# Stacks of the heads interleaved by four rows: six transfers of 256 KB in place of twelve of 128 KB, and the maxima's two rows in their free rows

## What is computed

```python
x = x + tanh(g_xattn[0]) * L0_xattn(layernorm(x), ctx, ...)    # two-way attention and a gate
x = x + tanh(g_ffn[0])   * L0_ffn(layernorm(x), ...)           # one expert of eight for each position
x = x + tanh(g_xattn[1]) * L1_xattn(layernorm(x), ctx, ctx)    # 16 heads, below
x = x + tanh(g_ffn[1])   * L1_ffn(layernorm(x), ...)           # two experts of eight, gelu

q, k, v = (heads(z @ W.T + b) for z in (x, ctx, ctx))          # 16 heads of 16 features
q = q * cos + rotate_half(q) * sin;  k = k * cos + rotate_half(k) * sin
p = softmax(q @ k.T * 16 ** -0.5)
out = merge(p @ v) @ Wo.T + bo
```

## Time and profile before

| | us |
|---|---|
| median of three runs | 536.92 |
| lowest and highest of them | 531.25, 536.98 |
| the profiled execution's own time | 531.52 |
| its span, first to last instruction | 530.2 |
| TensorE busy with matmuls | 469.8 (89% of the span) |
| VectorE, ScalarE, GpSimd busy | 346.1, 335.1, 280.8 |
| mean granted clock of TensorE | 0.941 of full speed |

### The profile page before, as it was taken

The page is one execution under the profiler, slowest core; times in us unless marked ns, Lnnn a source line. Parts: engine busy times, 40 slices in busy tenths (PEclk is TensorE's granted clock), DMA queues, the critical chain, the costliest instruction groups (busy, mean ns, idle before and its releaser), DMA issues.

```text
span 530.2 us, 11126 instructions
## 1 busy us (share of the span) xinstructions
PE 469.8 (89%) x3888; PEld 413.9 (78%) x3888; DVE 346.1 (65%) x865; ACT 335.1 (63%) x691; POOL 280.8 (53%) x362
## 2 busy tenths in 40 slices
PE   3999999999999674767886799999999999999996
PEld 3999999999888573636664558788788888878896
DVE  5576676787567557552645676868656695976475
ACT  3388788876758223322254578878867768687833
POOL 2236564575533876445366756837668184423154
PEclk9999999999999957777899579999999999999999
DMA  4679600015667415788768225051220602002001
GB/s 144 210 259 385 241 22 2 22 61 159 211 199 209 157 61 174 193 231 263 197 197 207 56 89 152 1 162 42 69 95 1 180 4 101 22 3 83 1 20 41
DMA packets 42635, 65.33 MB, mean 123 GB/s; under 512 B 6098, under 2 KB 23764, under 8 KB 42580
## 3 DMA queue, kind: packets, MB, share of 16 engines
q1 hardware_dynamic: 41044, 60.42, 37.4%
q0 software_dynamic: 1536, 4.20, 2.6%
HBM read 30.13 MB, written 17.43 MB: 90 GB/s over the span
## 4 chain that ended last, share of the span: by engine, by line
PE 61%; SPq 10%; DMA 8%; DVE 6%; issue 6%; POOL 5%; ACT 4%; POOLq 0%; DVEq 0%; ACTq 0%
PE psum L378 13%; PE psum L380 11%; PE psum L379 11%; SPq L2992 7%; PE psum L385 4%; PE psum L606 4%; PE psum L594 4%; DMA xs<-slots_d 3%; PE psum L577 3%; DMA st<-parts 3%; PE psum L543 2%; DMA y_d<-ys 2%; PE psum L510 1%; ACT PT L1346 1%; PE psum L419 1%
## 5 line engine op out<-in xcount | busy, mean ns | idle before, releaser
L2161 DVE TENSOR_REDUCE mpad<-psum 128x4 f32<-128x1024 f32 x64 | 76.4, 1220 | 23.9 <-PE psum L577 23.7
L1346 ACT ACTIVATE PT<-psum 128x1024 f32<-128x1024 f32 x64 | 63.7, 1026 | 17.6 <-PE psum L594 14.5
L2692 POOL TENSOR_TENSOR wA<-stage,wA 128x512 fp32r<-128x512 f32 x32 | 41.2, 1288 | 59.7 <-ACT wA L1393 57.1
L2230 DVE SCALAR_TENSOR_TENSOR xall<-psum,gat,xall 128x256 f32<-128x256 f32 x112 | 46.6, 474 | 9.7 <-PE psum L380 7.3
L577 PE MATMUL psum<-st 48*128 48x256 f32 x256 | 28.8, 331 | 12.3 <-DMA st<-parts 9.6
L378 PE MATMUL psum<-wB,wA 128*128 128x256 f32 x128 | 39.0, 304 | 0.1
L378 PE MATMUL psum<-x4h,wB 128*128 128x256 f32 x128 | 37.9, 296 | 0.1
L606 PE MATMUL psum<-PT,vv 128*32 128x256 f32 x512 | 36.0, 401 | 1.5 <-ACT PT L1346 1.5
L577 PEld LDWEIGHTS psum<-st 48*128 48x128 f32 x256 | 19.7, 202 | 21.9 <-DMA st<-parts 11.1
L2638 POOL TENSOR_SCALAR nm<-mv 128x2 f32<-128x2 f32 x32 | 7.7, 239 | 53.4 <-DVE mv L1926 41.8
L380 PE MATMUL psum<-x4h,wB 128*128 128x256 f32 x128 | 35.8, 280 | 0.0
(11 more groups left out here) (277 smaller groups left out, 1745.4 us busy)
## 6 DMA issues: line engine op xcount, KB each, us to landing
st<-parts SPq DMA_DIRECT2D x96, 128.0 KB, 3.1
wt<-exp_d SPq DMA_DIRECT2D x30, 384.0 KB, 3.9
slots_d<-ys SPq DMA_DIRECT2D x3, 2304.0 KB, 17.5
stage<-mats_d SPq DMA_DIRECT2D x21, 256.0 KB, 3.1
cx<-ctx_d SPq DMA_DIRECT2D x16, 256.0 KB, 4.5
qr<-qp SPq DMA_DIRECT2D x32, 128.0 KB, 2.6
xs<-slots_d SPq DMA_DIRECT2D x30, 128.0 KB, 4.0
y_d<-ys SPq DMA_DIRECT2D x30, 128.0 KB, 3.8
```

Of the source, the lines that this page charges most:

```text
L1346: e.activation(PT[:, i:i + 2, :, :].rearrange("p a k n -> p (a k n)"), ps2("ST", b, j).rearrange("p a n -> p (a n)"), ACT.Exp, scale=0.25) ...
L2161: e.tensor_reduce(mpad[:, :, 0:16].rearrange("p t (o a) -> p t o a", a=8)[:, :, :, j], ps2("max", b, j).rearrange("p o (t n) -> p t o n", ...
L2230: e.scalar_tensor_tensor(out=xall[:, b, t, :], in0=ps("dn", b, x)[:, t * 256:(t + 1) * 256], scalar=gat[:, b % 2, t, x:x + 1], in1=xall[:, ...
L2692: e.tensor_tensor(hlo[:, i, :], stage[:, n % 4, :], hh[:, i, :].bitcast(F32), ALU.subtract).then_inc(h_lo, 1)
```

## The change

`stack(b)` now copies each part of each side in one transfer over all 128 partitions. Row c + 4r of the tile holds part c of feature r, r counting through both halves, so each half of 64 rows has 16 groups of four rows of which the fourth is free. Six transfers of 256 KB replace twelve of 128 KB. The maxima's high row goes to the free row 63 of each half and the low row to 59: two transfers of 16 KB, each to both halves, replace four of 8 KB. Both sides of each tile are set over all 128 partitions at the start, side 0 to zero and side 1 to one, in place of 32 partitions twice.

`c_max` contracts 63 rows and `c_exp` 64. Row 59 is inside the 63, so it must be zero again when `c_max` reads the tile for the next sequence: `max_rows(b)` for b from 1 to 6 ends with a new transfer of zeros (16 KB, from `bo_r`) into row 59 of the other tile, once the exponents of sequence b - 1 have been formed (`t_ST`), and `c_max` of sequence b from 2 on has a second wait, for that transfer (`d_zero`). The other edits adjust counts of the same waits.

```diff
@@ c_max
-                w.wait_ge(d_stack, 192 * (b + 1))
+                w.wait_ge(d_stack, 96 * (b + 1))
+                if b >= 2:
+                    w.wait_ge(d_zero, 16 * (len(ZEROS) + b - 1))
                 for t in range(2):
                     for p in range(2):
-                        last = e.matmul(o[:, p, t * 256:(t + 1) * 256], s[64 * p:64 * p + 48, 0, j, t * 128:(t + 1) * 128],
-                                        s[64 * p:64 * p + 48, 1, j, :], start=True, stop=True)
+                        last = e.matmul(o[:, p, t * 256:(t + 1) * 256], s[64 * p:64 * p + 63, 0, j, t * 128:(t + 1) * 128],
+                                        s[64 * p:64 * p + 63, 1, j, :], start=True, stop=True)
@@ c_exp
-                w.wait_ge(d_mrow, 64 * (b + 1))
+                w.wait_ge(d_mrow, 32 * (b + 1))
-                        last = e.matmul(o[:, p, k * 256:(k + 1) * 256], s[64 * p:64 * p + 50, 1, j, k * 128:(k + 1) * 128],
-                                        s[64 * p:64 * p + 50, 0, j, :], start=True, stop=True)
+                        last = e.matmul(o[:, p, k * 256:(k + 1) * 256], s[64 * p:64 * p + 64, 1, j, k * 128:(k + 1) * 128],
+                                        s[64 * p:64 * p + 64, 0, j, :], start=True, stop=True)
@@ st0_init, and st1_init alike
-                for o in range(32, 128, 64):
-                    e.memset(st_[0][o:o + 32, 1, :, :].bitcast(F32), 1.0).then_inc(v_st, 1)
+                for side in range(2):
+                    e.memset(st_[0][:, side, :, :].bitcast(F32), float(side)).then_inc(v_st, 1)
@@ stack
                 for i, order in enumerate([(0, 1, 0), (0, 0, 1)]):
                     for c, p in enumerate(order):
-                        for o in range(2):
-                            e.dma_start(st_[b % 2][64 * o + c:64 * o + 48:3, i, :, :].bitcast(F32),
-                                        parts[p][64 * o:64 * o + 64, i, :, :].bitcast(F32)).then_inc(d_stack, 16)
+                        e.dma_start(st_[b % 2][c:128:4, i, :, :].bitcast(F32), parts[p][:, i, :, :].bitcast(F32)).then_inc(d_stack, 16)
@@ max_rows
-                w.wait_ge(d_mrow, 64 * b)
-                for o in range(2):
-                    for p in range(2):
-                        e.dma_start(st_[b % 2][64 * o + 48 + p:64 * o + 49 + p, 0, :, :].bitcast(F32), mpt[8 * o:8 * o + 8, p, :].bitcast(F32)).then_inc(d_mrow, 16)
+                w.wait_ge(d_mrow, 32 * b)
+                for p in range(2):
+                    e.dma_start(st_[b % 2][63 - 4 * p:128:64, 0, :, :].bitcast(F32), mpt[:, p, :].bitcast(F32)).then_inc(d_mrow, 16)
+                if 1 <= b < LAST:
+                    w.wait_ge(t_ST, 8 * b)
+                    e.dma_start(st_[(b + 1) % 2][59:128:64, 0, :, :].bitcast(F32), bo_r[32:48, :].bitcast(F32)).then_inc(d_zero, 16)
```

More of the change, by code:

```diff
@@ L1337, in part_hi @@
                 w.wait_ge(r_add, 2 * b + i + 1)
-                w.wait_ge(d_stack, 192 * b)
+                w.wait_ge(d_stack, 96 * b)
                 e.activation(parts[0][:, i, :, :], qp[:, i, :, :], ACT.Copy).then_inc(r_hi, 1)
@@ L2137, in st0_init @@
             def st0_init():
-                for o in range(32, 128, 64):
-                    e.memset(st_[0][o:o + 32, 1, :, :].bitcast(F32), 1.0).then_inc(v_st, 1)
+                for side in range(2):
+                    e.memset(st_[0][:, side, :, :].bitcast(F32), float(side)).then_inc(v_st, 1)
             def st1_init():
                 w.wait_ge(t_PV, 2 * NB)
-                for o in range(32, 128, 64):
-                    e.memset(st_[1][o:o + 32, 1, :, :].bitcast(F32), 1.0).then_inc(v_st, 1)
+                for side in range(2):
+                    e.memset(st_[1][:, side, :, :].bitcast(F32), float(side)).then_inc(v_st, 1)
             def turned(i):
```

## The result

The changed kernel took 536.04 us, the median of 20 runs (532.04 to 540.58), against 534.53 for the kernel before in as many (529.37 to 542.55). The ratio is 1.0092, with an interval of 1.0066 to 1.0117. Two later comparisons, each on one chip, gave 1.0012 [0.9957, 1.0066] and 0.9991 [0.9951, 1.0031]: a little slower or equal, within 2% in all three. Executions fall into a faster and a slower state; every ratio and interval here is taken over the faster ones of both kernels, so it is not the quotient of the medians, which is 1.0028, 1.0033 and 0.9994 in the three comparisons. The forecast was 537, in a range of 530 to 543.

The account below looks back on a forecast made before the run. Waits were taken to bound the early part, TensorE itself the late part. Zeros' waits of 5.2 us less gains of 3.45 gave +1.8: 533.3 against the profiled 531.5, 537 as the forecast time, range 530 to 543.

Parts of the forecast that it names:

- The late waits: At c_max(0, 6) and c_max(0, 7): waiting for zeros issued behind the maxima adds 1.8 and 2.7 us, counted in full.
- Rival 3: Zeros land under 1 us after issue; the late part costs 1.7 us, not 5.2; 533 as a median; chance 0.07.
- b = 5: At c_max(0, 5): the stack landing sooner covers nearly all of the 1.15 us wait; 1.15 us gained.
- a granted clock of 0.50 after 420: Sign in the late part: TensorE granted 0.50 after 420 us would show the forecast wrong.
- rival 2: New waits, deciding at c_max(0, 7), lower TensorE's clock: 17 us at half speed, 8.5 us more; 545 as a median; chance 0.14.
- b = 3 and 4: At c_max(0, 3) the zeros' wait replaces the stack's 0.73 us, +0.1 us; at c_max(0, 4) the zeros add 0.6 us.
- b = 2: At c_max(0, 2): engines are full and the zeros' wait allows 0.6 us at most; 0.3 us gained.
- b = 0 and 1: At c_max(0, 0) and c_max(0, 1): stack waits of 2.72 and 1.32 us shrink; 0.5 and 1.5 us gained.
- Rival 1: Wide transfers reach 346 GB/s even in a crowd, so early sequences gain 6.3 us; 534 as a median; chance 0.13.
- The landing of a wide transfer: Sign at the stack: a landing longer than 3.1 us after its last issue would show the forecast right.
- Edits at nothing: Contraction of 63 and 64 rows, the 128-partition fills and the zeros' wait for t_ST were each taken to cost 0.
- Engines per transfer: Maxima and zeros might use two engines, eight before; the sum would be 1 to 2 us higher, not counted.

Follow-up runs that it names:

- the kernel before with the wait: Kernel before plus a transfer of zeros into a row nothing reads, behind the maxima, and the wait for it ahead of c_max; 561.09 us, ratio 1.0653.

## Why the prediction was right, and where its steps were off

The call (within 2%) and the number held: 1.8 us over the profiled execution were forecast, a ratio of 1.003; the three comparisons gave 1.009, 1.001 and 0.999, and the profiled execution after was 3.1 us longer. The first comparison's interval (1.0066 to 1.0117) leaves out 1.003, so the change is known to be small and not how small. The cost of the zeros was forecast by its mechanism; that the sum came out so near is partly luck, since a term of the cost was missing and the gain was given to the wrong owner, both below.

- **The late waits** were right in place, cause and size. Forecast +1.8 and +2.7 at b = 6 and 7; the rows show 1.61 and 2.38, and the same within 0.01 in two more profiles. The landing, bounded at 2.1 from above by the earlier trace rows and from below only by the issue, is 2.1 (2.13 to 2.14 here). Rival 3, a landing under 1 us, is out.
- **b = 5** was right: the 1.15 us are gone in every profile of after. Together the late part should have grown by 1.8 + 2.7 - 1.15 = 3.35; it grew by 4.0. With the measured waits and the clock below it should even have been 1.61 + 2.38 + 1.7 - 1.15 = 4.5; another 0.5 us is gone between `c_max(0, 4)` and `c_max(0, 5)`, beside the wait there, and has no row of its own.
- **The missed term is the clock in the late part.** The text said that a granted clock of 0.50 after 420 would show it wrong, and rival 2 put its price at 8.5 us, with the wait at b = 7 deciding. It came, but for 3.4 us, 1.7 of lost work, and behind one of the two waits (b = 6 in two profiles, b = 7 in the third). Rival 2's mechanism is there; its size came from the wrong row: the 17 us of the earlier trace rows follow a wait of 3.64 in a stretch in which TensorE stood idle for 12 of 50 us, which the late part is not. Nor are they typical of that stretch: after a wait of 3.05 at the same `c_max(0, 2)`, with twelve transfers in the new places, 3.4 us of work were lost where the 17 us lost 8.5. The two terms of 1.6 and 2.4, with this 1.7, are the 5.7 us that the kernel without zeros saves.
- **b = 3 and 4**, forecast as waits of about 0.8 and 0.6 in all, show 0.72 to 1.22 and 0.54.
- **b = 2** rested on the new wait allowing 0.6 of gain at most; the waits of 1.87 to 2.85 there, with 0.43 when the zeros are gone, show that it was the zeros that bound it. The wait fell by 0.8 to 1.8, more than the 0.3 taken. But the wait of 3.64 is that of one execution: with one row of maxima in the kernel before there was none at b = 2.
- **b = 0 and 1**: their waits of 2.72 and 1.32 are gone, but what of it reached the end can't be read. I took 2 us for both as a gain of the wide transfers. With twelve narrow ones in the new places the wait at b = 1 is gone too (that at b = 0 is 0 and 0.29), and the total is within 0.8 us of that with six. So this part of the working named the wrong owner: the kernel with twelve transfers and no zeros is already 0.5 and 1.3% under the kernel before, and that gain belongs to the new places of the rows, which the prediction gave no price, or to the two fewer issues of maxima.
- **Rival 1**, wide transfers much faster in the crowd: in part. Without the zeros stack 2 was ready in 8.7 us from its first issue in place of 12.8 before and 11.3 with twelve transfers in new places. The whole did not move by it, so the time of 530.4 was not what it led to.
- **The landing of a wide transfer**, expected over 3.1 us as a sign of being right, was not longer: 2.4, 3.0 and 5.0 us (lowest, median, highest) in the changed kernel's third profile, against 2.7, 3.1 and 5.7.
- **Edits at nothing** held for the fills and the contraction. The fill of 128x2048 takes what 32x2048 did:

```profile
L2141 DVE MEMSET st<- x2: 1765/1765/1765, 1.2 to 3.4; 128x2048 f32 x2
L579 PE MATMUL psum<-st x256: 271/278/579, 226.0 to 476.3; 63*128 63x256 f32 x128
L2993 SPq DMA_DIRECT2D st<-parts x48: 575/610/1481, 216.1 to 446.8; - x48
L3002 SPq DMA_DIRECT2D st<-bo_r x6: 495/495/496, 295.1 to 454.1; - x6
```

The matmuls of 63 rows have the median of those of 48, 278 against 279 ns. From `c_max(0, 7)` to the end is 77.1 us before (530.2 - 453.14) and 77.1 without zeros (526.1 - 449.01), with eight `c_max` and more `c_exp` in it, so contraction rows cost nothing. An issue of 256 KB is 610 ns, against 601; the six took 3.8 to 4.8 us in the queue where 3.8 were forecast.
- **Engines per transfer.** From the Trainium skill, "DMA: Bandwidth & Descriptors", section "Why a DMA increments its semaphore by 16 and not by 1", and the page's rate of 27 GiB/s for an engine the prediction worked out an estimate of 1 to 2 us more, as a transfer over 2 partitions would use two engines. The trace does not bear the extra time out: at b = 6 and 7 the zeros, over 2 partitions, landed 2.1 us after the start of their issue, which is the bound seen for the maxima before, and the whole chain was 3.35 and 3.31 us, not above the 3.5 that the forecast had without it. How many engines served it is in no row.

**What stays open.** Why the new places with twelve transfers are faster than before: the stack lands sooner there, by 0.3 to 0.7 us at b = 3 and 5 and by 1.4 or more at b = 1 and 2, but what makes it land sooner is not shown. Two issues of maxima in place of four are not enough for the whole (1.0007 with two in the kernel before), though in the late part they give as much (172.3 in both). In the single profiles the rest goes with the clock: before and the second profile with twelve transfers are 4.6 us apart at `c_max(0, 4)` and 5.1 apart in the work lost to a low clock from 280 to 320. Whether the new places bring that, or chance, one profile of the kernel before can't say. Nor is it settled how much of the difference between 1.009 and 0.999 belongs to the chips.

## What to carry to other kernels

Before a free row of a tile is used twice, ask who cleans it and behind what in its queue: a transfer of 16 KB cost 1.3% by the ratios of two groups because it stood behind the maxima, and nothing that shows in the ratio (0.9879 with it and without) when it was issued ahead of the stack, where its condition had long been met. A wait that takes an independent step and ties it to a late one costs in full where the engine had no idle time; the rows of before (the start of the releaser, two issues, one landing) gave it to 0.3 us, and a low clock behind it came on top. A shorter queue is worth what its waits show and not its share of the chain: six issues fewer in each sequence moved the whole by 0.1 to 0.3%. A change of several things at once (width, rows, number of issues) needs a kernel for each before a gain is given to one of them.

## Not expected of the hardware

- A fall of the clock behind short waits in a busy stretch: after 1.61 us (or 2.38 in another execution) TensorE ran at 0.50 for 3.4 us and then at 1.00 again. At the waits of 5.78 and 3.56 in the kernel before with the wait it lasted 6.8 us, and behind that of 3.18 it did not come.
- In five of the fourteen profiles (after, twelve transfers, without zeros, and both with one row of maxima in one group) ScalarE and VectorE stood still together for some 3.5 us beside stack 2, and the release has no row of its own. In after:

```profile
284.86 1.23 DVE L2163 TENSOR_REDUCE mpad<-psum 128x4 f32<-128x1024 f32 x1 [3.46 <-remote]
284.86 1.02 ACT L1348 ACTIVATE PT<-psum 128x1024 f32<-128x1024 f32 x1 [3.44 <-remote]
```

Other profiles of the first four of these kernels do not have it, and it comes with narrow and with wide transfers alike. What stops there is not known, but it goes with the chip as far as is on record: the four profiles taken on one chip all have it, the eight on two other chips don't, and on which chip the first profiles of before and after were taken is not on record. Where it occurs, no wait for the stack shows at `c_max(0, 2)`. It is one reason why the early part can't be read from one profile.
